# Moving similarities and transpositions in a cluster-and-convolve kernel on one core

## The chip, the cores and the metric

The kernel runs on one core of one Trainium2 chip. The metric is the device time of one execution in microseconds (us), the median of several runs. Lower is better.

## The reference

Eight images of 512 channels and 32 x 48 = 1536 pixels. Each pixel is given to the centroid (of 40) with the largest cosine similarity; each image's clusters are averaged; each pixel is pulled toward the mean of its cluster by a weight from its squared distance; a 512 x 512 matrix is applied, a bias added and ReLU taken.

```
sim = einsum('bchw,nc->bnhw', x / |x|, centroids / |centroids|)
idx = argmax(sim, axis=1);  onehot = one_hot(idx, 40)
mean = einsum('bhwn,bchw->bnc', onehot, x) / max(count, 1)
delta = mean[b, idx] - x
alpha = exp(-mean_over_channels(delta * delta))
out = relu(einsum('oc,bchw->bohw', W, x + alpha * delta) + b)
```

## The kernel before, in words

Every image is cut into three units of 512 pixels, so there are 24 units g, with image b = g // 3 and position p = g % 3. Every engine has one instruction stream, written out by hand in the order in which the engine runs it; semaphores tie the streams together. An engine that waits holds back everything behind it in its stream.

From g = 3 on, one pass of the loop over g is called a slot. Slot g of TensorE (L978) holds: `gather(g, 0)` and `gather(g, 1)` (cluster means put back on the pixels of unit g, two banks of PSUM each), four `convolve(g-2, o)` (12 matmuls each) for the unit two slots back, and `sum_squares(g)` at its end. Beside that, the next image b+1 is prepared: in the first slot of an image (p = 0) the similarities of its units 0 and 1, in the second (p = 1) those of its unit 2 and `transpose_sims`, in the third (p = 2) its cluster sums, `transpose_onehot` and `add_halves`. A slot is measured here from the start of its `gather(g, 0)` to the next.

VectorE (DVE, L515) runs in each slot: `delta(g, 0)`, the two `scale(g-1, .)`, `delta(g, 1)`, three additions in `add_squares(g)`, `fold(g)`, `low_sum(g)`. Among them stand the work for the argmax (`best_sims`, `first_best`; p = 1), for the means (`low_clusters`, `counts`, `rest_of_mean`, `parts_of_mean`; p = 2), the two-part transpositions of pixels (`transpose_half(g+4, 0)` and `(g+4, 1)`, one unit a slot), and `second_rest` (p = 0 and 1), which with GpSimd's `first_rest` splits a transposed unit into bf16 parts for the cluster sums.

ScalarE (ACT, L701) squares, copies similarities (`copy_sims`), sums and one-hots, rounds y to its high part (`high_half`), moves the upper half of the squares' sum (`move_upper`), rounds the folded sum (`high_sum`) and applies `relu`. GpSimd (POOL, L328) runs for each unit `y_half` twice, `low_half` twice, and then, for two units of three, `first_rest(g+5)`. SyncE (SP, L265) issues in each slot `store(g-3)`, `load_x(g+5)` and `load_xs(g+6)`.

Waits that matter below: `convolve(g, o)` waits until `relu(g, o-2)` has freed its half of `main` (L874); `gather(g, 1)` waits for `delta(g, 0)` (L847); `gather(g, 0)` for `add_squares(g-1)` and for the means; `transpose_half` for the cluster sums that still read the buffer it writes, and for its load; `load_xs(g)` for the transposition of unit g-2, and `load_x(g)` for `y_half` of unit g-6.

Of the kernel before, what the change touches and what calls it, by code (L numbers as in the profile page):

```python
# [21 lines left out]
Q = 4  # L22
# [13 lines left out]

SPLIT = 2

DIRECT = 2


def wait(eng, sem, value):
    if value > 0:
        eng.wait_ge(sem, value)
# [16 lines left out]


def split(g):
    return g >= 2 * PARTS and g % PARTS < SPLIT


def splits(g):
# [14 lines left out]
def build(nc, x, cent, w, bias, out):  # L82
# [3 lines left out]
    with ctx:  # L86
# [55 lines left out]

        main, gat, fa = ps("main", [P, 2, UNIT]), ps("gat", [P, 2, UNIT]), ps("fa", [P, 2, UNIT])
        al, sumP = ps("al", [P, UNIT]), ps("sump", [P, UNIT])
        simP = [fa[:, 0, 0:256], fa[:, 1, 0:256], fa[:, 0, 256:512]]
        simT = fa[:, :, :].rearrange("p a (s h n) -> p (a s h) n", h=2, n=NPAD)[:, 0:PARTS * TILES, 0:N]
        first = fa[:, 1, 384:384 + PARTS * TILES]
        ohP = fa[:, :, :].rearrange("p a n -> p (a n)").bitcast(BF16)
        def mean(b):
            return al[0:NK, :] if b == 0 else fa[0:NK, 0, :]  # L150

        def alpha(g):
            return gat[:, 0, :] if g == 1 else al[:, :]
# [30 lines left out]
        block = ctx.enter_context(nc.Block())  # L184

        def wT(k):
            return (main[:, 0, :], main[:, 1, :], gat[:, 0, :], gat[:, 1, :])[k]

        def span(g):
            return slice(g % PARTS * UNIT, (g % PARTS + 1) * UNIT)  # L190
# [146 lines left out]
        def _(dve):  # L337
            v_ = nc.vector

            def keep_transposed():  # L340
                dve.wait_ge(xp_done, 1)
                v_.tensor_copy(XT[:, 0, 0:HALF, :], main[:, :, :]).then_inc(xe_dve, 1)

            def transpose_half(g, h):
                M = C // BLK
# [70 lines left out]
            def add_squares(g):  # L416
                upper = squares(g, 1)
                dve.wait_ge(sq_done, 2 * g + 2)
                v_.tensor_tensor(SQ[:, 0, :], SQ[:, 0, :], upper[:, 0, :], ALU.add).then_inc(pair_done, 1)
                v_.tensor_tensor(upper[:, 1, :], SQ[:, 1, :], upper[:, 1, :], ALU.add).then_inc(pair_done, 1)  # L420
                dve.wait_ge(pair_done, 2 * folded(g))
                wait(dve, za_done, 2 * g)
                v_.tensor_tensor(al[:, :], SQ[:, 0, :], upper[:, 1, :], ALU.add).then_inc(s_done, 1)

            def fold(g):
# [53 lines left out]
            keep_transposed()  # L479
            best_sims(0)  # L480
            first_best(0)
            for k in range(KC):
                low_weights(k)
            transpose_half(3, 0)
            low_clusters(0)
            transpose_half(3, 1)
            counts(0)
            rest_of_mean(0)
            parts_of_mean(0)

            for g in range(DIRECT):
                delta(g, 0)
# [22 lines left out]
            for g in range(PARTS, UNITS):  # L515
                b, p = divmod(g, PARTS)
                beside = b + 1 < BATCH
                delta(g, 0)
                if g == PARTS:
                    transpose_half(g + 3, 0)  # L520
                    transpose_half(g + 3, 1)
                scale(g - 1, 0)
                scale(g - 1, 1)
                delta(g, 1)
                y_half(g - 1, 1)
                if beside and p < 2:
                    transpose_half(g + 4, 0)
                if beside and p == 2:
                    low_clusters(b + 1)
                    counts(b + 1)  # L530
                add_squares(g)
                if beside and p == 0:
                    transpose_half(g + 4, 1)
                fold(g)
                if beside and p == 2:
                    rest_of_mean(b + 1)
                if beside and p == 1:
                    best_sims(b + 1)
                low_sum(g)
                low_half(g - 1, 1)  # L540
                if beside and p == 1:
                    first_best(b + 1)
                    transpose_half(g + 4, 1)
                if beside and p == 2:
                    parts_of_mean(b + 1)
                    if g + 4 < UNITS:
                        transpose_half(g + 4, 0)
                        transpose_half(g + 4, 1)
                if g + 3 < UNITS and split(g + 3):
                    second_rest(g + 3)  # L550
            g = UNITS - 1
# [6 lines left out]
        def _(act):  # L558
            a_ = nc.scalar

            def keep_transposed(u, half):
                act.wait_ge(xp_done, 2 * u + half + 1)
                a_.activation(XT[:, u, HALF * half:HALF * (half + 1), :], (main, gat)[half][:, :, :],
                              ACT.Copy).then_inc(xe_act, 1)

            def square(g, h):
# [36 lines left out]
            def copy_sims(g):  # L603
                b, u = divmod(g, PARTS)
                act.wait_ge(sims_done, g + 1)
                wait(act, simT_done, b)
                dst, src = simS[:, u, :, :].rearrange("p t s -> p (t s)"), simP[u]
                if not plain(b):
                    dst = simS[:, u, :, :].rearrange("p t (q i) -> p q t i", q=Q)
                    src = simP[u].rearrange("p (q t i) -> p q t i", q=Q, t=HALF)  # L610
                a_.activation(dst, src, ACT.Copy, scale=cstat[:, 6:7]).then_inc(simS_done, 1)

            def copy_onehot(b):
# [51 lines left out]
            high_weights(0)  # L665
            high_weights(1)
            copy_onehot(0)
            high_weights(2)
            high_weights(3)
            copy_sums(0)  # L670
            evacuate_onehot(0)
            scale_means(0)
            high_means(0)
            act.wait_ge(b_in, 16)
            copy_sims(3)
            copy_sims(4)
# [24 lines left out]
            for g in range(PARTS, UNITS):  # L701
                b, p = divmod(g, PARTS)
                beside = b + 1 < BATCH
                if g > PARTS:
                    relu(g - 3, 3)
                    exp(g - 1)
                square(g, 0)
                if beside and p == 2:
                    copy_sums(b + 1)
                    evacuate_onehot(b + 1)  # L710
                    high_half(g - 1, 0)
                    square(g, 1)
                    high_half(g - 1, 1)
                    relu(g - 2, 0)
                    scale_means(b + 1)
                    move_upper(g)
                    high_means(b + 1)
                    high_sum(g)
                    relu(g - 2, 1)
                else:  # L720
                    relu(g - 2, 0)
                    if g == PARTS:
                        exp(g - 1)
                    square(g, 1)
                    if beside:
                        copy_sims(3 * b + 3 + 2 * p)
                    high_half(g - 1, 0)
                    if beside and p == 0:
                        copy_sims(3 * b + 4)
                    if not beside:  # L730
                        relu(g - 2, 1)
                    move_upper(g)
                    if not beside:
                        high_sum(g)
                    high_half(g - 1, 1)
                    if beside:
                        high_sum(g)
                        relu(g - 2, 1)
                relu(g - 2, 2)
                if beside and p == 1:  # L740
                    copy_onehot(b + 1)
# [13 lines left out]
        def _(pe):  # L755
            t_ = nc.tensor

            def similarities(g):
                b, u = divmod(g, PARTS)
                pe.wait_ge(x_in[b % 2][u], 16 * (b // 2 + 1))  # L760
                if b == 1:
                    pe.wait_ge(ohT_done, 1)
                wait(pe, g_ready, b if b > 1 else 0)
                if u == 2:
                    pe.wait_ge(simS_done, PARTS * b + 1)
                rows = X[b % 2]
                for k in range(KC):
                    for h in range(2):
# [2 lines left out]
                            toks = toks[:, h * HALF * P:(h + 1) * HALF * P]  # L771
                        else:
                            toks = toks.rearrange("p (q s) -> p q s", q=Q)[:, :, h * HALF * BLK:(h + 1) * HALF * BLK]
                        last = t_.matmul(simP[u][NPAD * h:NPAD * (h + 1), :], cT[:, k, :], toks,  # L774
                                         start=(k == 0), stop=(k == KC - 1))
                last.then_inc(sims_done, 1)

# [60 lines left out]
            def gather(g, h):  # L838
# [1 line left out]
                pe.wait_ge(g_ready, b + 1)  # L840
                pe.wait_ge(ohT_done, b + 1)
                if g == 0:
                    pe.wait_ge(wl_done, KC)
                elif g < DIRECT:
                    pe.wait_ge(z_done, 2 * (g - 1) + h + 1)
                elif h == 1:
# [40 lines left out]
            def transpose_x(u, half):  # L887
# [4 lines left out]
                for t in range(HALF):  # L892
                    at = u * UNIT + (HALF * half + t) * P
                    for k in range(KC):
                        last = t_.transpose((main, gat)[half][:, t, k * P:(k + 1) * P], X[0][:, k, at:at + P],
                                            ident[:, :])
                last.then_inc(xp_done, 1)

# [38 lines left out]
            transpose_weights(1)  # L937
            pe.wait_ge(const_done, 8)
            sum_clusters(0, 0)
            transpose_weights(2)  # L940
            transpose_weights(3)
            sum_clusters(0, 1)
            sum_clusters(0, 2)
            transpose_onehot(0)
            add_halves(0)

            similarities(3)
            similarities(4)
# [29 lines left out]
            for g in range(PARTS, UNITS):  # L978
# [3 lines left out]
                if beside and p == 2:  # L982
                    for u in sum_order(b + 1):
                        sum_clusters(b + 1, u)
                    gather(g, 1)
                    transpose_onehot(b + 1)
                    convolve(g - LAG, 0)
                    add_halves(b + 1)
                else:
                    convolve(g - LAG, 0)  # L990
                    if g == PARTS:
                        sum_squares(g - 1)
                    gather(g, 1)
                    if beside and p == 0:
                        similarities(3 * b + 3)
                        similarities(3 * b + 4)
                    if beside and p == 1:
                        similarities(3 * b + 5)
                convolve(g - LAG, 1)
                if beside and p == 1:  # L1000
                    transpose_sims(b + 1)
# [26 lines left out]
```

## Time and profile before

| | us |
|---|---|
| median of 3 runs (424.49 to 428.45) | 424.5 |
| the profiled execution | 424.58 |
| its span, first to last instruction | 422.8 |
| TensorE busy | 412.9 (98%) |
| VectorE busy | 344.3 (81%) |
| GpSimd busy | 263.5 (62%) |
| ScalarE busy | 256.4 (61%) |

The profiled execution took 424.58 us, 1.8 us more than its span. Busy shares are means over the whole run; a full engine is one that has no gap in the stretch looked at, and what an engine waited for stands in the table of waits.

### The profile page before, as it was taken

What the parts mean: (1) busy time and instruction counts of PE and PEld (TensorE: products, weight loads), DVE (VectorE), ACT (ScalarE), POOL (GpSimd) and SP (SyncE); (2) the same over time, 40 slices, a digit from 0 to 9 for tenths busy, and PEclk for the clock granted to TensorE, in tenths of its full rate; (3) what the DMA queues carried; (4) which work ended last, traced back from release to release, by engine and by line L of the source; (5) the groups of instructions that cost most, each with busy time, mean ns of one, the idle gap of its engine ahead of it and who ended that gap; (6) DMA issues with size and microseconds to landing.
All of it is one profiled execution on the core that took longest, in us unless ns stands there. A gap on an engine that the chain in (4) does not pass through costs nothing.

```text
span 422.8 us, 5887 instructions
## 1 busy us (share of the span) xinstructions
PE 412.9 (98%) x2154; PEld 293.7 (69%) x2154; DVE 344.3 (81%) x412; ACT 256.4 (61%) x351; POOL 263.5 (62%) x114
## 2 busy tenths in 40 slices
PE   8999999799999999999999999999999999999996
PEld 6744466575867757776777758677677758777885
DVE  2468979889799888998799997998899997788730
ACT  5665374565855666655855657747655658566641
POOL 2000655993879946995869936997669938334320
PEclk9999999899999999999999999999999999999999
DMA  8997295966669473994859674893858220222223
GB/s 276 314 292 130 51 253 153 273 169 182 215 183 240 176 200 109 258 231 142 236 119 274 175 191 160 205 292 99 207 146 246 99 101 1 101 99 99 90 79 130
DMA packets 70927, 73.94 MB, mean 175 GB/s; under 512 B 2724, under 2 KB 45732, under 8 KB 70900
## 3 DMA queue, kind: packets, MB, share of 16 engines
q1 hardware_dynamic: 70900, 73.58, 62.2%
q8 instruction: 17, 0.28, 0.3%
q14 instruction: 10, 0.08, 0.1%
HBM read 48.40 MB, written 25.17 MB: 174 GB/s over the span
## 4 chain that ended last, share of the span: by engine, by line
PE 90%; POOL 2%; DVE 2%; ACT 2%; DMA 1%; issue 1%; SPq 0%
PE main L880 20%; PE main L881 19%; PE main L882 19%; PE sump L823 9%; PE fa L774 9%; PE gat L855 5%; DMA x<-x 1%; PE fa L783 1%; PE al L862 1%; POOL z L310 1%; PE fa L798 1%; PE main L923 1%; DVE xt L350 1%; PE al L868 1%; PE gat L868 1%
## 5 line engine op out<-in xcount | busy, mean ns | idle before, releaser
L880 PE MATMUL main<-yh,wh 128*128 128x512 f32 x376 | 153.4, 408 | 2.6 <-ACT o L600 2.6
L881 PE MATMUL main<-yl,wh 128*128 128x512 f32 x376 | 147.6, 392 | 0.0
L882 PE MATMUL main<-yh,wl 128*128 128x512 f32 x376 | 147.4, 392 | 0.0
L317 POOL TENSOR_TENSOR yl<-z,yh 128x1024 fp32r<-128x1024 f32 x44 | 105.6, 2421 | 55.3 <-ACT yh L592 55.3
L310 POOL TENSOR_TENSOR z<-z,x 128x1024 f32<-128x1024 f32 x42 | 99.8, 2397 | 62.2 <-DVE z L437 62.2
L600 ACT ACTIVATE o<-main,bcol 128x512 f32<-128x512 f32 x96 | 65.0, 681 | 63.7 <-PE main L882 63.6
L880 PEld LDWEIGHTS main<-yh,wh 128*128 128x128 f32 x376 | 71.0, 189 | 23.9 <-issue 5.0
L882 PEld LDWEIGHTS main<-yh,wl 128*128 128x128 f32 x376 | 71.0, 189 | 15.3
L881 PEld LDWEIGHTS main<-yl,wh 128*128 128x128 f32 x376 | 71.0, 189 | 13.9
L324 POOL TENSOR_TENSOR xr<-xt 128x2048 f32<-128x2048 f32 x12 | 57.4, 4786 | 24.2 <-DVE xt L350 24.2
L413 DVE TENSOR_TENSOR z<-gat,x 128x1024 f32<-128x1024 f32 x46 | 56.2, 1222 | 7.5 <-PE gat L855 7.4
L592 ACT ACTIVATE yh<-z 128x1024 fp32r<-128x1024 f32 x48 | 50.6, 1054 | 10.0 <-POOL z L310 8.6
L437 DVE TENSOR_TENSOR z<-z,al 128x1024 f32<-128x1024 f32 x46 | 54.0, 1215 | 0.5 <-ACT al L587 0.5
L350 DVE STREAM_TRANSPOSE xt<-xs 128x1024 f32<-128x1024 f32 x42 | 51.0, 1230 | 0.4 <-DMA xs<-x 0.4
L774 PE MATMUL fa<-x,c_t 128*64 128x256 f32 x384 | 45.2, 383 | 0.5 <-ACT oht L623 0.3
L358 DVE TENSOR_TENSOR xr<-xr 128x2048 bf16<-128x2048 f32 x12 | 43.9, 3658 | 0.2
L574 ACT ACTIVATE sq<-z 128x1024 f32<-128x1024 f32 x22 | 23.3, 1061 | 26.4 <-DVE z L413 26.4
L774 PEld LDWEIGHTS fa<-x,c_t 128*64 128x64 f32 x384 | 26.7, 137 | 17.8 <-issue 6.9
L574 ACT ACTIVATE gat<-z 128x1024 f32<-128x1024 f32 x22 | 22.6, 1026 | 20.6 <-DVE z L413 20.6
L823 PE MATMUL sump<-xt,oh 128*64 128x512 f32 (+1 forms) x144 | 31.5, 532 | 0.0
L855 PE MATMUL gat<-oht,g 128*128 128x512 bf16 x92 | 27.9, 385 | 0.6 <-DVE g L406 0.6
L427 DVE TENSOR_TENSOR al<-upper_sum,al 64x512 f32<-64x512 f32 x22 | 15.0, 680 | 11.2 <-ACT upper_sum L578 11.2
(118 smaller groups left out, 380.0 us busy)
## 6 DMA issues: line engine op xcount, KB each, us to landing
x<-x SPq DMA_DIRECT2D x24, 1024.0 KB, 5.5
out<-o SPq DMA_DIRECT2D x23, 1024.0 KB, 6.1
xs<-x SPq DMA_DIRECT2D x84, 256.0 KB, 5.6
o<-w SPq DMA_DIRECT2D x1, 1024.0 KB, 12.1
out<-o SPq DMA_DIRECT2D x4, 256.0 KB, 2.1
sq<-centroids SPq DMA_DIRECT2D x2, 80.0 KB
bcol<-bias SPq DMA_DIRECT2D x1, 2.0 KB, 11.6
```

The source lines that it names most:

```text
L310: pool.tensor_tensor(z, z, X[g // PARTS % 2][:, pair(h), span(g)], ALU.add).then_inc(y_pool, 1)
L317: pool.tensor_tensor(YL[g % 2][:, pair(h), :], Z[g % 2][:, pair(h), :], YH[g % 2][:, pair(h), :].bitcast(F32), ALU.subtract).then_inc(lo_p ...
L324: pool.tensor_tensor(XR[:, g % PARTS, :, :].rearrange("p t c -> p (t c)"), xt.rearrange("p t c -> p (t c)"), halfword(xt, 1), ALU.subtract ...
L350: last = v_.transpose(XT[:, g % PARTS, :, :].rearrange("p t (m j) -> p m t j", j=BLK)[:, blocks, :, :], XS[g % 2][:, blocks, :])
L413: v_.tensor_tensor(Z[g % 2][:, pair(h), :], banks(g, h)[:, :, :], X[g // PARTS % 2][:, pair(h), span(g)], ALU.subtract).then_inc(z_done, 1)
L437: v_.tensor_tensor(z, z, alpha(g).unsqueeze(1).to_broadcast([P, 2, UNIT]), ALU.mult).then_inc(za_done, 1)
L600: a_.activation(OUT[g % 2][:, o, :], main[:, o % 2, :], ACT.Relu, bias=bcol[:, o:o + 1]).then_inc(relu_done, 1)
L774: last = t_.matmul(simP[u][NPAD * h:NPAD * (h + 1), :], cT[:, k, :], toks, start=(k == 0), stop=(k == KC - 1))
L823: last = t_.matmul(sumP[NPAD * h:NPAD * (h + 1), :], onehot[:, slot(u, tile), :], x_part[:, tile * C:(tile + 1) * C], start=(opens and t = ...
L880: t_.matmul(main[:, o % 2, :], WH[:, k, rows], YH[g % 2][:, k, :], start=(k == 0), stop=False)
L881: t_.matmul(main[:, o % 2, :], WH[:, k, rows], YL[g % 2][:, k, :], start=False, stop=False)
L882: last = t_.matmul(main[:, o % 2, :], WL[:, k, rows], YH[g % 2][:, k, :], start=False, stop=(k == KC - 1))
```

## The change

- From image 3 on (`AHEAD` = 9), `similarities` of unit 0 of an image run one image earlier, in the third slot between the cluster sums and `gather(g, 1)`, into the bank `al` instead of `fa`. TensorE waits for `za_done` (both `scale(g-1, .)`) before them. ScalarE's `copy_sims` of that unit stands behind `copy_sums`, and VectorE's last addition of `add_squares` waits for that copy.
- From image 3 on, the similarities of units 1 and 2 run together in the second slot, ahead of `gather(g, 1)`; none are left in the first slot. In ScalarE's second slot `copy_sims(g+3)`, `high_half(g-1, 0)`, `copy_sims(g+4)` now stand ahead of `square(g, 1)`.
- VectorE's transpositions for g+3 >= 9: none in the first slot; both halves of unit g+4 ahead of `delta(g, 1)` in the second; units g+4 and g+5 (four halves) after `parts_of_mean` in the third.
- In the first slot of every image `relu(g-2, 1)` now stands ahead of `high_sum(g)`.
- Unit 6 is no longer split (`split(g)` asks g > 6): its `first_rest` and `second_rest` go, and its cluster sums run in f32.
- At the start, the transpositions of weight blocks 2 and 3 run behind the first image's cluster sums, with ScalarE's and VectorE's copies moved accordingly; blocks 0 and 1 use `gat`, 2 and 3 `main`, and the first `gather` waits for two weight blocks instead of four.

```diff
+AHEAD = 3 * PARTS
 def split(g):
-    return g >= 2 * PARTS and g % PARTS < SPLIT
+    return g > 2 * PARTS and g % PARTS < SPLIT
+        def simP(g):
+            if g >= AHEAD and g % PARTS == 0:
+                return al[:, 0:256]
+            return (fa[:, 0, 0:256], fa[:, 1, 0:256], fa[:, 0, 256:512])[g % PARTS]
...
             # VectorE, add_squares
+                if AHEAD <= g + 4 < UNITS and g % PARTS == 2:
+                    dve.wait_ge(simS_done, g + 5)
                 v_.tensor_tensor(al[:, :], SQ[:, 0, :], upper[:, 1, :], ALU.add).then_inc(s_done, 1)
...
             # VectorE, slots
                 scale(g - 1, 1)
+                if beside and p == 1 and g + 3 >= AHEAD:
+                    transpose_half(g + 4, 0)
+                    transpose_half(g + 4, 1)
                 delta(g, 1)
                 y_half(g - 1, 1)
-                if beside and p < 2:
+                if beside and p < 2 and g + 3 < AHEAD:
                     transpose_half(g + 4, 0)
...
                 add_squares(g)
-                if beside and p == 0:
+                if p == 0 and g + 3 < AHEAD:
                     transpose_half(g + 4, 1)
                 fold(g)
...
                     parts_of_mean(b + 1)
                     if g + 4 < UNITS:
                         transpose_half(g + 4, 0)
                         transpose_half(g + 4, 1)
+                        if g + 5 >= AHEAD:
+                            transpose_half(g + 5, 0)
+                            transpose_half(g + 5, 1)
...
             # ScalarE, slots
                     copy_sums(b + 1)
+                    if AHEAD <= g + 4 < UNITS:
+                        copy_sims(g + 4)
                     evacuate_onehot(b + 1)
...
+                    elif beside and p == 1:
+                        copy_sims(g + 3)
+                        high_half(g - 1, 0)
+                        copy_sims(g + 4)
+                        square(g, 1)
...
                     move_upper(g)
                     high_half(g - 1, 1)
+                    if beside and p == 0:
+                        relu(g - 2, 1)
                     if beside:
                         high_sum(g)
+                    if beside and p == 1:
                         relu(g - 2, 1)
...
             # TensorE, similarities and slots
+                if g >= AHEAD and u == 0:
+                    pe.wait_ge(za_done, 2 * (g - PARTS - 1))
...
                         sum_clusters(b + 1, u)
+                    if AHEAD <= g + 4 < UNITS:
+                        similarities(g + 4)
                     gather(g, 1)
...
+                    if beside and p == 1 and g + 3 >= AHEAD:
+                        similarities(g + 3)
+                        similarities(g + 4)
                     gather(g, 1)
...
             # TensorE, start
             sum_clusters(0, 0)
-            transpose_weights(2)
-            transpose_weights(3)
             sum_clusters(0, 1)
             sum_clusters(0, 2)
             transpose_onehot(0)
+            transpose_weights(2)
             add_halves(0)
+            transpose_weights(3)
```

## Rows read from the trace of the kernel before

**Rows 1.** Waits of TensorE, whole run: us in total, times, longest us.

```profile
PE main L880 <- ACT o L600: 2.6, 1, 2.6
```

**Rows 2.** Busy time by window, the columns PE, PEld, DVE, ACT, POOL, clock, DMA.

```profile
80.80:85.40 4.60, 4.60 (x13) 3.48 (x13) 4.57 (x2) 0.49 (x1) 4.60 (x2) 0.63 1.12 316
...
197.70:246.30 48.60, 48.60 (x261) 34.91 (x259) 43.85 (x47) 30.69 (x43) 37.85 (x14) 1.00 0.72 195
```

**Rows 3.** The chain that ended last, 195 to 250 us: start, us, what.

```profile
197.71 0.45 PE gat L855 x2
...
202.74 0.54 PE gat L855 x2
...
215.64 0.45 PE gat L855 x2
...
219.28 3.60 PE fa L774 x32
...
231.51 0.45 PE gat L855 x2
...
235.15 1.88 PE fa L774 x16
...
246.33 0.45 PE gat L855 x2
```

**Rows 4.** Waits of VectorE from 197.7 to 246.3 us.

```profile
DVE z L413 <- PE gat L855: 0.3, 1, 0.3
```

**Rows 5.** Timeline of VectorE, slots 11 to 13: start, us, instruction.

```profile
200.21 1.20 DVE L413 TENSOR_TENSOR z<-gat,x 128x1024 f32<-128x1024 f32 x1
...
213.09 0.75 DVE L406 SCALAR_TENSOR_TENSOR g<-part,cols,fa 128x512 bf16<-128x512 bf16 x1
213.76 2.37 DVE L350 STREAM_TRANSPOSE xt<-xs 128x1024 f32<-128x1024 f32 x2
...
219.53 1.22 DVE L413 TENSOR_TENSOR z<-gat,x 128x1024 f32<-128x1024 f32 x1
...
226.25 0.68 DVE L431 TENSOR_TENSOR shl<-al,shl 64x512 fp32r<-64x512 f32 x1 [0.66 <-ACT shl L583]
226.97 4.75 DVE L358 TENSOR_TENSOR xr<-xr 128x2048 bf16<-128x2048 f32 x1
...
235.39 1.22 DVE L413 TENSOR_TENSOR z<-gat,x 128x1024 f32<-128x1024 f32 x1
...
246.37 2.56 DVE L358 TENSOR_TENSOR xr<-xr 128x2048 bf16<-128x2048 f32 x1
```

**Rows 6.** Timeline of ScalarE, slots 12 and 13.

```profile
223.89 0.60 ACT L578 ACTIVATE upper_sum<-al 64x512 f32<-64x512 f32 x1 [0.30 <-DVE al L423]
...
241.82 0.67 ACT L600 ACTIVATE o<-main,bcol 128x512 f32<-128x512 f32 x1
```

**Rows 7.** Timeline of GpSimd, slot 12.

```profile
216.21 3.60 POOL L324 TENSOR_TENSOR xr<-xt 128x2048 f32<-128x2048 f32 x1 [4.10 <-DVE xt L350]
...
224.46 4.75 POOL L317 TENSOR_TENSOR yl<-z,yh 128x1024 fp32r<-128x1024 f32 x2
229.17 5.97 POOL L324 TENSOR_TENSOR xr<-xt 128x2048 f32<-128x2048 f32 x1
```

**Rows 8.** Timeline, all engines, slot 3.

```profile
72.21 1.22 DVE L413 TENSOR_TENSOR z<-gat,x 128x1024 f32<-128x1024 f32 x1
...
73.67 4.77 POOL L310 TENSOR_TENSOR z<-z,x 128x1024 f32<-128x1024 f32 x2
...
80.77 0.50 PE L880 MATMUL main<-yh,wh 128*128 128x512 f32 x1 [2.58 <-ACT o L600]
```

**Rows 9.** Timeline of TensorE, start of the run.

```profile
22.05 1.09 PE L916 MATMUL gat<-ident,o 128*128 128x128 f32 x8
23.07 3.65 PE L823 MATMUL sump<-xt,oh 128*64 128x512 f32 x16
```

**Rows 10.** DMA issues of the page: KB each, median us to landing.

```profile
x<-x SPq DMA_DIRECT2D x24, 1024.0 KB, 5.5
```

More of the change, by code:

```diff
@@ L144, in build @@
         al, sumP = ps("al", [P, UNIT]), ps("sump", [P, UNIT])
-        simP = [fa[:, 0, 0:256], fa[:, 1, 0:256], fa[:, 0, 256:512]]
         simT = fa[:, :, :].rearrange("p a (s h n) -> p (a s h) n", h=2, n=NPAD)[:, 0:PARTS * TILES, 0:N]
@@ L186, in wT @@
         def wT(k):
-            return (main[:, 0, :], main[:, 1, :], gat[:, 0, :], gat[:, 1, :])[k]
+            return (gat[:, 0, :], gat[:, 1, :], main[:, 0, :], main[:, 1, :])[k]
         def span(g):
@@ L341, in keep_transposed @@
                 dve.wait_ge(xp_done, 1)
-                v_.tensor_copy(XT[:, 0, 0:HALF, :], main[:, :, :]).then_inc(xe_dve, 1)
+                v_.tensor_copy(XT[:, 0, 0:HALF, :], gat[:, :, :]).then_inc(xe_dve, 1)
             def transpose_half(g, h):
@@ L481, in _ @@
             first_best(0)
-            for k in range(KC):
-                low_weights(k)
+            low_weights(0)
+            low_weights(1)
             transpose_half(3, 0)
@@ L487, in _ @@
             counts(0)
+            low_weights(2)
             rest_of_mean(0)
             parts_of_mean(0)
+            low_weights(3)
             for g in range(DIRECT):
@@ L542, in _ @@
                     first_best(b + 1)
-                    transpose_half(g + 4, 1)
+                    if g + 3 < AHEAD:
+                        transpose_half(g + 4, 1)
                 if beside and p == 2:
@@ L562, in keep_transposed @@
                 act.wait_ge(xp_done, 2 * u + half + 1)
-                a_.activation(XT[:, u, HALF * half:HALF * (half + 1), :], (main, gat)[half][:, :, :],
+                a_.activation(XT[:, u, HALF * half:HALF * (half + 1), :], (gat, main)[half][:, :, :],
                               ACT.Copy).then_inc(xe_act, 1)
@@ L606, in copy_sims @@
                 wait(act, simT_done, b)
-                dst, src = simS[:, u, :, :].rearrange("p t s -> p (t s)"), simP[u]
+                dst, src = simS[:, u, :, :].rearrange("p t s -> p (t s)"), simP(g)
                 if not plain(b):
                     dst = simS[:, u, :, :].rearrange("p t (q i) -> p q t i", q=Q)
-                    src = simP[u].rearrange("p (q t i) -> p q t i", q=Q, t=HALF)
+                    src = simP(g).rearrange("p (q t i) -> p q t i", q=Q, t=HALF)
                 a_.activation(dst, src, ACT.Copy, scale=cstat[:, 6:7]).then_inc(simS_done, 1)
@@ L667, in _ @@
             copy_onehot(0)
-            high_weights(2)
-            high_weights(3)
             copy_sums(0)
             evacuate_onehot(0)
+            high_weights(2)
             scale_means(0)
             high_means(0)
+            high_weights(3)
             act.wait_ge(b_in, 16)
@@ L723, in _ @@
                         exp(g - 1)
-                    square(g, 1)
-                    if beside:
+                    if g + 3 < AHEAD:
+                        square(g, 1)
                         copy_sims(3 * b + 3 + 2 * p)
-                    high_half(g - 1, 0)
-                    if beside and p == 0:
-                        copy_sims(3 * b + 4)
+                        high_half(g - 1, 0)
+                        if p == 0:
+                            copy_sims(3 * b + 4)
+                    elif beside and p == 1:
+                        copy_sims(g + 3)
+                        high_half(g - 1, 0)
+                        copy_sims(g + 4)
+                        square(g, 1)
+                    else:
+                        square(g, 1)
+                        high_half(g - 1, 0)
                     if not beside:
@@ L762, in similarities @@
                     pe.wait_ge(ohT_done, 1)
-                wait(pe, g_ready, b if b > 1 else 0)
+                if g >= AHEAD and u == 0:
+                    pe.wait_ge(za_done, 2 * (g - PARTS - 1))
+                else:
+                    wait(pe, g_ready, b if b > 1 else 0)
                 if u == 2:
@@ L773, in similarities @@
                             toks = toks.rearrange("p (q s) -> p q s", q=Q)[:, :, h * HALF * BLK:(h + 1) * HALF * BLK]
-                        last = t_.matmul(simP[u][NPAD * h:NPAD * (h + 1), :], cT[:, k, :], toks,
+                        last = t_.matmul(simP(g)[NPAD * h:NPAD * (h + 1), :], cT[:, k, :], toks,
                                          start=(k == 0), stop=(k == KC - 1))
@@ L842, in gather @@
                 if g == 0:
-                    pe.wait_ge(wl_done, KC)
+                    pe.wait_ge(wl_done, KC // 2 * (h + 1))
                 elif g < DIRECT:
@@ L894, in transpose_x @@
                     for k in range(KC):
-                        last = t_.transpose((main, gat)[half][:, t, k * P:(k + 1) * P], X[0][:, k, at:at + P],
+                        last = t_.transpose((gat, main)[half][:, t, k * P:(k + 1) * P], X[0][:, k, at:at + P],
                                             ident[:, :])
@@ L992, in _ @@
                         sum_squares(g - 1)
+                    if beside and p == 1 and g + 3 >= AHEAD:
+                        similarities(g + 3)
+                        similarities(g + 4)
                     gather(g, 1)
[L994 to L998, printed above, removed]
+                    if p == 0 and g + 3 < AHEAD:
+                        similarities(g + 3)
+                        similarities(g + 4)
+                    if p == 1 and g + 3 < AHEAD:
+                        similarities(g + 4)
                 convolve(g - LAG, 1)
```

## The prediction

> **What bounds the kernel now.** First the table of TensorE's waits: it waits in earnest once, 2.6 us [rows 1], so from the first slots to the end the time is the sum of its matmuls. Then the windows of one image, slots 11 to 13: TensorE busy in all of 48.60 us, at the full clock, VectorE in 43.85 [rows 2]. That looks like 4.8 us to spare on VectorE, and the next view takes it back: in those 48.6 us VectorE waits for TensorE only 0.3 us, at one `delta` [rows 4]. The rest of its idle time it waits for ScalarE, which in those places works on what VectorE gave it a moment before; this is a chain that no faster TensorE shortens. So VectorE's stream with its hand-overs to ScalarE is nearly as long as TensorE's. The change leaves the work of both as it is and moves it; the question is whether VectorE still fits.
>
> **The slots by TensorE alone.** From the chain [rows 3]: the third slot 215.64 - 197.71 = 17.9 us, the first 231.51 - 215.64 = 15.9, the second 246.33 - 231.51 = 14.8, together 48.6. Two units of similarities cost 3.60, one unit 1.88. After the change TensorE would need 17.9 + 1.9 = 19.8 in the third slot, 15.9 - 3.6 = 12.3 in the first, 14.8 - 1.9 + 3.6 = 16.5 in the second: the same 48.6. Nothing is gained there; waits can only be added. VectorE has the most to do in the first and second slots.
>
> **The third slot after.** VectorE enters it 200.21 - 197.71 = 2.5 us late, busy with `second_rest` [rows 3, 5]. Its `delta` and two `scale` take 3.4 (from the end of the transpositions at 213.76 + 2.37 = 216.13 to the next `delta` at 219.53 [rows 5]). The added wait of TensorE for the second `scale` ends at 2.3 + 3.4 = 5.7 into the slot (2.3 is the lateness that comes out below), while the cluster sums are done at 202.74 - 197.71 = 5.0 [rows 3]: 0.7 us of waiting, with `gather(g, 1)`, the one-hot transpositions and all convolutions queued behind. What follows on ScalarE and VectorE starts from these, so it shifts by 1.9 + 0.7 = 2.6, as does the slot's end: 20.5 us. `parts_of_mean` now ends about 213.84 - 197.71 = 16.1 in [rows 3, 5], then at 18.7, still 1.8 before the slot's end. ScalarE's added copy lies in the time in which it waits for the one-hots, and VectorE's added wait for that copy is over long before: nothing for both. The early similarities need their pixels: these are issued after `y_half` in the second slot, some 10 us in by the walk below, and land 5.5 later [rows 10], before the third slot begins. Nothing for that. The transposed loads of SyncE are no later, since the transpositions that release them come earlier or in the same place.
>
> **The first slot after** (t from its start). VectorE has four halves of transpositions instead of two behind `parts_of_mean`: 4 x 1.18 = 4.7 (2.37 for two [rows 5]), from t = -1.8 to 2.9. Now `delta(g, 0)` comes at 2.9 instead of 0.5, and `gather(g, 1)`, due at 3.2, waits until 4.1. `delta(g, 1)` starts at 2.9 + 3.4 = 6.3. From there to `move_upper` it is 223.89 - 219.53 = 4.4 [rows 5, 6]. Before, two halves of transpositions lay in this stretch, yet their removal shortens nothing: they lay beside ScalarE's square and move, which now show as waits of VectorE. `move_upper` starts at 10.7; behind it in ScalarE's stream stand `high_half` and then `relu(g-2, 1)`, together to 12.8 (0.6, 1.05 and 0.68, less overlaps of their starts; in slot 13 `move_upper`, `high_half`, `high_sum` and this `relu` end 7.1 after `delta(g, 1)`, 241.82 + 0.67 - 235.39 [rows 5, 6], of which `high_sum` is 0.6). Convolution 3 waits for that `relu`. By TensorE it would be due at 10.0, so it waits 2.8, and the slot ends after it and `sum_squares`, 3.0 later: 15.9 us instead of 12.3. The 3.6 us taken out of the slot come back whole.
>
> Meanwhile VectorE does `low_sum` to 14.05 and then `second_rest`. In the trace that takes 2.56 alone and 4.75 when GpSimd is in its `low_half` [rows 5]: there it ended at 231.72, 2.55 after GpSimd's pair ended at 224.46 + 4.75 = 229.2, and GpSimd's `first_rest`, begun then, took 5.97 instead of 3.60 [rows 7]. The two take turns. GpSimd here has `first_rest` from 0.6 to 4.2, two `y_half` to 9.9, two `low_half` (2.37 each, half of 4.75) to 14.7. So `second_rest` ends at 14.7 + 2.55 = 17.25, 1.4 into the second slot.
>
> **The second slot after.** `delta`, `scale` and two halves of transpositions (5.8) bring VectorE to 7.2; `gather(g, 1)`, now behind 3.6 of similarities, gives `delta(g, 1)` at 7.3 instead of 3.9. `relu(g-2, 1)` here still stands behind `high_sum`, so it ends 7.1 later, at 14.4. Convolution 3 is due at 13.6: it waits 0.8, and the slot is 17.4. The argmax and `second_rest` (alone, 2.56) end 19.7 in, so 2.3 into the third slot, which closes the circle.
>
> One image: 20.5 + 15.9 + 17.4 = 53.8 against 48.6, or 5.2 more. Five images run so (third slots 5 to 17, with the first and second after each): 5 x 5.2 = +26.
>
> **The start.** In slot 3 GpSimd's `first_rest(6)` kept `y_half(2)` off until 73.67, its `high_half` and a `relu` came behind, and TensorE waited 2.58 until 80.77 [rows 8]. Without it, and with `relu` ahead of `high_sum`, the limit is ScalarE's stream: `delta` at 72.21 [rows 8] + 4.4 + 2.1 = 78.75, 2.0 earlier; I take 1.9. In the 4.6 us behind the wait the clock was 0.63 of full [rows 2]: matmuls at 1.2 GHz for most of it, 4.6 x 0.37 = 1.7 lost. I take that back, as 0.7 us of waiting remains; bounds 0 and 1.7. Unit 6 in f32: two f32 units 3.65 [rows 9], so 1.85 a unit; the sums of three units now 202.74 - 198.16 = 4.6 [rows 3], so 1.37 a split unit: +0.5. The weight transpositions took 23.07 - 22.05 = 1.0 between cluster sums [rows 9]; moved behind them, they let the first means come earlier, less a weight copy of 0.55 on ScalarE in the same path. I take 0.7, bounds 0 and 1.0. Sum: -1.9 - 1.7 + 0.5 - 0.7 = -3.8.
>
> **The clock.** Each first slot after has a wait of about 2.8 us, near to the one of 2.58 behind which the clock fell, at a cost of 1.7 [rows 1, 2]. Whether each of the five does so, one row can't tell: 0 to 1.7 each; I take half, +4. Total: 424.6 - 3.8 + 26 + 4 = 451 us. The median equals the profiled run within 0.1 us.
>
> **Rivals.**
> - VectorE fits, and TensorE stays the bound: only the start counts, 424.6 - 3.8 = 420.8, faster by 0.9%. For it: TensorE's work is unchanged, and 4.8 us of VectorE stand idle in an image [rows 2]. Against it: the four halves would have to end by about the first slot's start, so `parts_of_mean` 4.2 before it, and it ends 1.8 before. Chance 0.07.
> - VectorE's lateness is absorbed, and only the order on GpSimd and ScalarE binds. `first_rest` ends at 4.2 into the first slot, the second `y_half` at 8.9, `high_half` and `relu` at 10.6; convolution 3, due at 9.1, waits 1.5. With 0.8 in the second slot and 0.7 in the third it is 3.0 an image: 420.8 + 15 = 436. Chance 0.15.
> - The turns of `second_rest` and `first_rest` go the other way. If the second `low_half` ends before `low_sum` (0.6 us of margin above), GpSimd starts `first_rest` (3.6) and VectorE waits for all of it: 20.2 instead of 17.25, which puts `delta(g, 1)` of the second slot 2.9 later: 5 x 2.9 = 14.5, so 465. Chance 0.1. The Trainium skill (SBUF — State Buffer, Who interferes with whom) says that a VectorE instruction with two SBUF inputs contends with a GpSimd one that reads SBUF, and that issue order decides who blocks, wholly. By that rule, this rival is decided by which is first, and the turns in the trace agree.
> - The forecast, with both ends of the clock's cost: 447 to 456. Chance 0.65; 0.03 is left for what I do not see.
>
> From the second rival's 436, less 2 for the start's bounds, to 461, between the forecast's end and the third rival, the range holds 8 in 10. A change under 1% can hardly be told from none here. Faster than that: 0.04, half of the first rival and a little of the start's bounds; within 1%: 0.05; slower: 0.91.
>
> **What would show it.** Right: chain pieces of `gather` that make first slots near 15.9 us, not 12.3; TensorE waits of 2 to 3 us at convolution 3 behind a `relu`, five times; VectorE without a wait for TensorE in the first slot; its `delta(g, 0)` there some 3 us after the slot's start; slot 3 shorter by about 3.6. Wrong: images of 48.6 us, a `delta` in the first slot that waits for `gather`, or third slots much beyond 20.5, which would mean pixels that come late. The weakest links are 2.8 us of waiting (it decides on the clock) and the turns of the two bf16 splits.

## The result and the profile after

The changed kernel takes 453.2 us, median of 6 runs (450.8 to 455.9), against 424.8 us for the kernel before, run beside it: a ratio of 1.065, 95% interval 1.060 to 1.070. The forecast was 451, the range 434 to 461. The profiled execution is the fastest of the six, 450.77 us with a span of 449.0.

TensorE's waits, whole run (us in total, times, longest), answer to [rows 1]:

```profile
PE main L917 <- ACT o L619: 19.2, 11, 2.7
PE gat L892 <- DVE z L420: 3.6, 5, 0.7
PE al L810 <- DVE z L447: 2.7, 5, 0.7
```

One wait of 2.6 us has become 21 waits, in three places, each once an image for five images: `convolve` for `relu` (eleven: one in slot 3, and two an image), `gather(g, 1)` for a late `delta`, and the early similarities for the second `scale`.

Two images by window, slots 8 to 10 and 11 to 13 (TensorE, its weight loads, VectorE, ScalarE, GpSimd, clock, DMA share, GB/s), answer to [rows 2]:

```profile
150.90:204.90 54.00, 48.73 (x255) 35.12 (x259) 42.33 (x47) 30.36 (x43) 37.80 (x14) 1.00 0.65 175
204.90:260.40 55.50, 50.21 (x255) 36.18 (x259) 42.46 (x47) 30.39 (x43) 37.79 (x14) 0.97 0.65 174
```

54.0 us instead of 48.6 for the same matmuls; TensorE stands idle 5.3. No engine is full any more: here the time goes along a chain that passes from engine to engine. The second image took 1.5 more at a lower clock.

TensorE's timeline, the starts of `gather(g, 0)` of slots 8 to 11 and the waits between (start, us, instruction), answers to [rows 3]:

```profile
150.91 0.38 PE L892 MATMUL gat<-oht,g 128*128 128x512 bf16 x1
...
156.39 1.95 PE L810 MATMUL al<-x,c_t 128*64 128x256 f32 x16 [0.52 <-DVE z L447]
...
171.29 0.38 PE L892 MATMUL gat<-oht,g 128*128 128x512 bf16 x1
...
175.13 0.59 PE L892 MATMUL gat<-oht,g 128*128 128x512 bf16 x2 [0.72 <-DVE z L420]
...
183.84 0.50 PE L917 MATMUL main<-yh,wh 128*128 128x512 f32 x1 [2.65 <-ACT o L619]
...
187.16 0.38 PE L892 MATMUL gat<-oht,g 128*128 128x512 bf16 x1
...
201.62 0.50 PE L917 MATMUL main<-yh,wh 128*128 128x512 f32 x1 [1.05 <-ACT o L619]
...
204.94 0.38 PE L892 MATMUL gat<-oht,g 128*128 128x512 bf16 x1
```

The third slot takes 171.29 - 150.91 = 20.4, the first 15.9, the second 17.8. The first slot holds 3.6 us less work than before and is as long as before.

VectorE's timeline through that first slot, from the transpositions behind `parts_of_mean` on, answers to [rows 5]:

```profile
169.26 4.61 DVE L357 STREAM_TRANSPOSE xt<-xs 128x1024 f32<-128x1024 f32 x4
173.80 1.18 DVE L420 TENSOR_TENSOR z<-gat,x 128x1024 f32<-128x1024 f32 x1
174.91 2.33 DVE L447 TENSOR_TENSOR z<-z,al 128x1024 f32<-128x1024 f32 x2
177.17 1.21 DVE L420 TENSOR_TENSOR z<-gat,x 128x1024 f32<-128x1024 f32 x1
179.47 0.69 DVE L426 TENSOR_TENSOR sq<-sq,gat 128x512 f32<-128x512 f32 x1 [1.10 <-ACT gat L593]
...
182.16 0.69 DVE L437 TENSOR_TENSOR al<-upper_sum,al 64x512 f32<-64x512 f32 x1 [0.66 <-ACT upper_sum L597]
...
184.29 0.68 DVE L441 TENSOR_TENSOR shl<-al,shl 64x512 fp32r<-64x512 f32 x1 [1.45 <-ACT shl L602]
185.01 3.10 DVE L365 TENSOR_TENSOR xr<-xr 128x2048 bf16<-128x2048 f32 x1
```

The four halves end 2.5 us after the slot's start, the first `delta` begins there instead of 0.5 in, and the two places where halves of transpositions lay before, beside ScalarE's square and move, now show as VectorE's waits (1.10 and 0.66). The third wait, 1.45, is for `high_sum`, ahead of which a `relu` now stands. ScalarE's and GpSimd's lines of the same slot, answers to [rows 6] and [rows 7]:

```profile
181.53 0.59 ACT L597 ACTIVATE upper_sum<-al 64x512 f32<-64x512 f32 x1 [1.11 <-DVE al L433]
182.03 1.04 ACT L611 ACTIVATE yh<-z 128x1024 fp32r<-128x1024 f32 x1
183.10 0.69 ACT L619 ACTIVATE o<-main,bcol 128x512 f32<-128x512 f32 x1
```

```profile
180.92 4.67 POOL L324 TENSOR_TENSOR yl<-z,yh 128x1024 fp32r<-128x1024 f32 x2
185.56 5.97 POOL L331 TENSOR_TENSOR xr<-xt 128x2048 f32<-128x2048 f32 x1
```

The `relu` that ends at 183.79 is what convolution 3 waited for, and it stood behind `move_upper`, which waited 1.11 for VectorE's last addition.

### The profile page after: what moved, and what is told of

Same layout as the page of the kernel before. It is cut to its first block, busy times and chain, and to the rows that moved or that the text cites. A ratio compares the mean times of both kernels' runs of the same rounds, so it can differ in the third digit from the quotient of the medians.

```text
span 449.0 us, 5849 instructions
## 1 busy us (share of the span) xinstructions
PE 413.7 (92%) x2123; PEld 294.8 (66%) x2150; DVE 332.2 (74%) x411; ACT 254.4 (57%) x351; POOL 257.4 (57%) x113
## 4 chain that ended last, share of the span: by engine, by line
PE 47%; DVE 28%; ACT 13%; issue 10%; DMA 1%; SPq 0%; ACTq 0%; DVEq 0%
PE main L917 9%; PE main L918 8%; PE main L919 8%; PE fa L810 7%; DVE z L447 6%; DVE xt L357 5%; ACT yh L611 5%; DVE z L420 5%; PE sump L859 3%; ACT gat L593 3%; PE gat L892 3%; DVE xr L365 3%; PE al L810 2%; DVE al L433 2%; DVE gat L427 2%
## 5 line engine op out<-in xcount | busy, mean ns | idle before, releaser
L917 PE MATMUL main<-yh,wh 128*128 128x512 f32 x376 | 156.2, 415 | 19.2 <-ACT o L619 19.2
L918 PEld LDWEIGHTS main<-yl,wh 128*128 128x128 f32 x376 | 71.5, 190 | 13.9
L331 POOL TENSOR_TENSOR xr<-xt 128x2048 f32<-128x2048 f32 x11 | 51.4, 4675 | 23.9 <-DVE xt L357 23.9
L357 DVE STREAM_TRANSPOSE xt<-xs 128x1024 f32<-128x1024 f32 x42 | 49.4, 1219 | 2.6 <-DMA xs<-x 2.6
L810 PE MATMUL fa<-x,c_t 128*64 128x256 f32 x304 | 35.5, 383 | 0.8 <-DMA x<-x 0.8
L365 DVE TENSOR_TENSOR xr<-xr 128x2048 bf16<-128x2048 f32 x11 | 31.2, 2835 | 0.2
L426 DVE TENSOR_TENSOR sq<-sq,gat 128x512 f32<-128x512 f32 x22 | 15.1, 686 | 20.6 <-ACT gat L593 20.6
L810 PEld LDWEIGHTS fa<-x,c_t 128*64 128x64 f32 x304 | 21.0, 137 | 13.6 <-issue 4.3
L892 PE MATMUL gat<-oht,g 128*128 128x512 bf16 x65 | 21.7, 381 | 6.6 <-DVE z L420 3.6
```

The lines of the kernel that those rows point to most:

```text
L357: last = v_.transpose(XT[:, g % PARTS, :, :].rearrange("p t (m j) -> p m t j", j=BLK)[:, blocks, :, :], XS[g % 2][:, blocks, :])
L810: last = t_.matmul(simP(g)[NPAD * h:NPAD * (h + 1), :], cT[:, k, :], toks, start=(k == 0), stop=(k == KC - 1))
L917: t_.matmul(main[:, o % 2, :], WH[:, k, rows], YH[g % 2][:, k, :], start=(k == 0), stop=False)
L918: t_.matmul(main[:, o % 2, :], WH[:, k, rows], YL[g % 2][:, k, :], start=False, stop=False)
```

## Experiments

Times are medians; each is beside runs of the kernel before on the same chip (424.6 to 424.8).

**The two halves of the change, apart and without both.** Four kernels make a square: neither (`start_only`), similarities alone, transpositions alone, and the changed kernel with both.

```diff
-AHEAD = 3 * PARTS
+AHEAD = UNITS          # start_only
```

> Keeps the change at the start, unit 6 unsplit and relu ahead of high_sum in first slots; similarities and transpositions stay where they were. My theory: the start is worth 3.8 us and nothing else is left, 420.8 us. Rival (the loss sits in what this kernel keeps, such as the order of relu in every first slot): above 430.

421.1 us (ratio 0.992, 0.990 to 0.993): TensorE's only wait for another engine beyond the start is 0.7 us in slot 3. So what the changed kernel loses comes from the two moves.

```diff
+MOVED = UNITS          # sims_only; the conditions on VectorE's transpositions test MOVED for AHEAD
...
+AHEAD = UNITS          # transpositions_only
+MOVED = 3 * PARTS
```

> The changed kernel with the transpositions where they were. Theory (late VectorE is one half of the loss): the first slot falls from 15.9 to 13.8 (convolution 3 waits 1.5 behind relu, second y_half and first_rest), the second stays at 17.8, the third waits 1.5 for the second scale and takes 21.3; 52.9 an image, 420.8 + 5 x 4.3 = 442. Rival A (the four halves are the whole cause): 421 to 424. Rival B (they are no cause): 450.

445.8 us (1.050, 1.049 to 1.052). TensorE's waits:

```profile
PE main L918 <- ACT o L620: 16.4, 11, 1.6
PE al L811 <- DVE z L448: 5.6, 5, 1.2
PE sump L860 <- DVE xt L358: 1.7, 5, 0.3
```

The convolutions of the first slot wait 1.57, as expected from `first_rest` and `y_half`, but those of the second 1.6 and not 1.05: there `square(g, 1)` stands behind `high_half(g-1, 0)`, and GpSimd is late with the `y_half` that this one needs. So the similarities alone cost 24.7 us over `start_only`, 3.5 more than I had worked out.

> The changed kernel with the similarities where they were, transpositions moved. Theory: third slot 17.9; first slot 15.9 + 0.9 (gather 1 waits for a late delta) = 16.8 with no wait at convolution 3; second slot: delta 1 at 6.3 instead of 3.9, convolution 3 waits 1.6, 16.4; 51.1 an image, 420.8 + 5 x 2.5 = 433. Rival A (transpositions alone do it): about 450. Rival B (similarities alone do it): 421.

433.6 us (1.022, 1.020 to 1.023). The slots take 17.9, 16.7 and 16.6, close to what was expected, but the waits are not all those named: convolution 3 of the second slots waits 0.8 and not 1.6, and `transpose_sims` waits 0.4 for ScalarE's copy.

```profile
PE main L918 <- ACT o L620: 4.8, 6, 0.8
PE gat L893 <- DVE z L421: 3.5, 5, 0.7
PE fa L820 <- ACT sims L631: 2.0, 5, 0.4
```

Transpositions alone cost 12.5, similarities alone 24.7, both 32.1 (453.2 - 421.1). But in the last number the clock fell, and in the other two it stayed full. In the profiled execution of the changed kernel these falls cost 2.8 us; without them both moves cost 450.8 - 2.8 - 421.1 = 26.9, and the parts, 37.2 together, are 10 us more than the whole, since the same slots are late in both. The image of slots 8 to 10 says the same: 48.6 us with neither move (145.70 to 194.32), 51.2 with the transpositions (147.75 to 198.94), 53.7 with the similarities (149.62 to 203.34), 54.0 with both. The similarities are most of the loss. On top of them the transpositions add little to an image; they lengthen the longest wait from 1.6 to 2.65 us, and it is behind such waits that the clock fell. So the rivals that put all on the transpositions fall, and so does the one that put nothing on them when they are moved alone. The rival of `sims_only` that they are no cause, 450, is off by 4.2, and the theory's 442 by 3.8: that run alone does not tell them apart.

**Is the order on ScalarE the cause?**

```diff
-                    if not beside:
+                    if not beside or g + 3 >= AHEAD:
                         relu(g - 2, 1)
                     move_upper(g)
...                  # the later call of this relu goes in these slots
```

> The changed kernel with relu(g-2, 1) ahead of move_upper in the first and second slots of images 3 to 7, so that convolution 3 no longer waits behind VectorE's additions. Theory (VectorE's chain is the bound, relu is only where TensorE feels it): first slot 13.1, but VectorE then starts the second slot 4 us late, and it and the third slot take back what was won; 53.5 an image, 448 to 450. Rival (the order on ScalarE is the cause): 2.7 + 1.05 us saved in each of five images, 432.

445.4 us (1.049, 1.048 to 1.051); the image takes 53.6 us (148.40 to 202.02), as expected, and 421 + 5 x 4.9 gives 445. The 448 to 450 was reckoned from the changed kernel's median, in which falls of the clock are contained; here the clock stayed full. TensorE now waits for VectorE by name:

```profile
PE sump L859 <- DVE oh L386: 7.5, 5, 1.5
PE al L810 <- DVE z L447: 6.1, 5, 1.4
PE gat L892 <- DVE z L420: 3.5, 5, 0.7
PE al L899 <- DVE shl L441: 2.4, 5, 0.5
```

3.7 us of waits for `relu` an image are gone, and the image is 0.4 us shorter: TensorE stands idle 4.7 us of it instead of 5.3, most of that in these four places. Of the 7.8 us between the two medians about 5 are falls of the clock that are gone. The order on ScalarE was where TensorE felt the chain; VectorE was the chain.

**Ahead of the gather, or behind it?** Similarities moved, transpositions not, but the similarities run behind `gather(g, 1)`.

```diff
+                    gather(g, 1)
                     if AHEAD <= g + 4 < UNITS:
                         similarities(g + 4)
-                    gather(g, 1)
```

(The same in the second slot, and there `square(g, 1)` ahead of the copies on ScalarE.)

> As sims_only (similarities moved, transpositions where they were), but in the third and second slots the similarities run behind gather(g, 1), and square(g, 1) ahead of their copies. Theory (what costs in the similarities' move is that VectorE waits for a gather that stands behind them): second slot 16.5 without a wait at convolution 3, first slot 13.8, third 20.6; 50.9 an image, 420.8 + 11.7 = 433. Rival A (unequal slots alone cost it, the place within the slot does not matter): 445. Rival B (the place is all of it): 421.

431.8 us (1.017, 1.015 to 1.018). Of the 24.7 us that the similarities cost alone, 14 go with the place within the slot. VectorE's waits for a gather, whole run, first in `sims_only`, then here:

```profile
DVE z L421 <- PE gat L893: 30.6, 15, 2.7
...
DVE z L421 <- PE gat L893: 8.1, 7, 2.6
```

So the matmuls ahead of the gather were a wait of VectorE for its `delta`. What the order on ScalarE, changed with it, has in the 14 was not separated. Most of the rest is the first slot, which takes 13.9 us, since convolution 3 still waits 1.57:

```profile
PE main L918 <- ACT o L620: 8.6, 6, 1.6
```

**That last wait, with `relu` ahead of `move_upper` in first slots.**

> As sims_behind_gather, with relu(g-2, 1) ahead of move_upper in first slots, so that convolution 3 there (1.57 us of waiting in each of five) is free. Theory: VectorE and GpSimd begin the second slot later by the same amount; its convolution 3 waits about 0.8: 427. Rival (the wait was the order on ScalarE alone): 431.8 - 7.9 = 424.

434.3 us (1.021, 1.019 to 1.024): slower than without it, and neither number was right. The wait left convolution 3 and came back larger, in a place that I had not reckoned with:

```profile
PE gat L891 <- DVE z L421: 9.8, 5, 2.0
```

With a first slot of 12.05 us VectorE comes out of `second_rest` so late, 3.9 us into the second slot (184.50 - 180.61), that `gather(g, 1)` there waits for `delta(g, 0)`. At the full clock nothing is won or lost by that: three slots take 50.8 us (168.57 to 219.36), as in `sims_behind_gather` (147.23 to 197.99). What makes this kernel slower is the clock, which fell behind two of the five waits: those second slots take 20.4 and 20.3 us instead of 18.7, a loss of 3.3 us; less 1.0 won in slot 3 that makes 2.3 of the 2.5 us between the medians.

**The terms of the start.** The kernel before with one part each: unit 6 unsplit; `relu` ahead of `high_sum` in first slots; weights' transpositions moved.

> The kernel before with unit 6 unsplit, nothing else. Theory (first_rest of unit 6 on GpSimd held the chain of slot 3): relu of slot 3 still behind high_sum, 0.5 later than in the changed kernel, so convolution 3 waits 1.25 instead of 2.6; the clock does not fall (1.7); f32 sums cost 0.5: 424.6 - 2.5 = 422.1. Rival (the order of relu was the cause): 425.

> The kernel before with relu(g-2, 1) ahead of high_sum in first slots, nothing else. Theory: with first_rest still ahead of y_half in slot 3, the wait there shrinks by 0.6 to about 2.0; all other first slots had no wait. 424.0, or 422.3 if the clock does not fall behind the shorter wait. Rival (the order of relu was the cause): 421.5.

> The kernel before with the moved transpositions of weights, nothing else. Theory: first gather 0.7 earlier, but slot 3 begins only 0.5 earlier: 424.0 to 424.1. Rival (hidden by the chain through VectorE): 424.6.

422.4 (0.994, 0.993 to 0.996), 424.2 (0.999, 0.998 to 1.000) and 424.0 us (0.998, 0.998 to 0.999): -2.3, -0.5 and -0.7, together the -3.5 of `start_only`. In `split_only` the wait in slot 3 is 1.4 us and the clock stays full; in `relu_only` it is 2.1 and the clock still falls, in 9 of 11 executions by their mean clocks.

**A faster start.** What is left in slot 3 is 0.7 us for a `relu`; ahead of `move_upper` it should go.

```diff
-                    if not beside:
+                    if not beside or p == 0:      # start_relu_early; g == PARTS: start_relu_slot3
                         relu(g - 2, 1)
                     move_upper(g)
...                  # the later call of this relu goes in these slots
```

> As start_only, with relu(g-2, 1) ahead of move_upper in first slots. Theory: the last 0.74 us of waiting in slot 3 goes, all other slots have no wait: 420.4. Rival (VectorE's chain in slot 3 gives it back): 421.1.

424.7 us: 3.6 slower than `start_only`, against both expectations. `start_relu_early_look` is the same kernel once more, for its trace (424.6 us), and `start_relu_slot3` has the edit in slot 3 alone.

> start_relu_early once more, for its trace. Theory: relu, now ahead of move_upper, waits for convolution 1, which runs behind 3.6 us of similarities in the first slot; so move_upper, fold and low_sum come some 2 us later, GpSimd has started first_rest before VectorE reaches second_rest, and VectorE waits for all of it; gather(g, 1) of the second slot then waits for a late delta. 424.7, with second_rest ending 2.5 us after first_rest. Rival: the loss is in slot 3 alone.

> As start_only, with relu(g-2, 1) ahead of move_upper in slot 3 alone, where no second_rest follows. Theory: 0.7 us of waiting goes, 420.4. Rival (the loss of start_relu_early is in slot 3): 424.

`start_relu_slot3`: 420.0 us (0.989, 0.987 to 0.990), the fastest of all; its interval just meets that of `start_only`. So the loss is in the other first slots. ScalarE, VectorE and GpSimd in one of them, slot 12, which starts at 212.66:

```profile
223.05 0.69 ACT L619 ACTIVATE o<-main,bcol 128x512 f32<-128x512 f32 x1 [2.17 <-PE main L917]
223.77 0.60 ACT L597 ACTIVATE upper_sum<-al 64x512 f32<-64x512 f32 x1
```

```profile
224.40 0.69 DVE L437 TENSOR_TENSOR al<-upper_sum,al 64x512 f32<-64x512 f32 x1 [2.20 <-ACT upper_sum L597]
...
226.68 3.62 DVE L365 TENSOR_TENSOR xr<-xr 128x2048 bf16<-128x2048 f32 x1
```

```profile
225.39 2.41 POOL L324 TENSOR_TENSOR yl<-z,yh 128x1024 fp32r<-128x1024 f32 x1 [1.26 <-ACT yh L611]
227.75 5.97 POOL L331 TENSOR_TENSOR xr<-xt 128x2048 f32<-128x2048 f32 x1
```

Half of the theory holds: with similarities behind the gather, convolution 1 is late, `relu` waits 2.17 for it in front of everything else on ScalarE, and VectorE's `fold` waits 2.20 behind that. The other half does not: `second_rest` still got its turn before `first_rest`. VectorE enters the second slot at 230.3, 1.8 late, and TensorE waits 0.2 at a convolution there and 0.3 at the cluster sums of the third slot, in five images:

```profile
PE sump L857 <- DVE xt L357: 1.6, 5, 0.3
PE main L915 <- ACT o L619: 1.1, 5, 0.2
```

These waits add up to 2.7 us, and the slots show more. From one first slot to the next it is 49.6 us (178.95 to 228.53) and not 48.6 (179.50 to 228.12): second slots are 0.55 longer and third ones 0.42, 4.8 in five images. Slot 3, from the `sum_squares` before it to its own, is 1.05 shorter, which leaves 3.8, against 3.6 between the medians. A wait in these tables counts from the end of the matmul before, as the profile models it: `start_only` shows 0.74 in slot 3, and the slot is 1.05 shorter without it.

## Why the prediction was right, step by step

- TensorE as the bound of the kernel before, with VectorE just below it: right. `start_only` runs the old slots with no wait behind slot 3, and each kernel that moved similarities or transpositions takes 11 to 32 us more than it, with the same matmuls for TensorE.
- Third slot 20.5: measured 20.4. The wait for `scale` was put at 0.7 and is 0.5.
- First slot 15.9: measured 15.9. `gather(g, 1)` was to wait 0.9, and waits 0.7; convolution 3 was to wait 2.8, and waits 2.65. That the sum is exact is luck: `relu` ends 12.5 into the slot and not 12.8, and what stands behind it takes 3.4 and not 3.0.
- Second slot 17.4: measured 17.8, with 1.05 of waiting at convolution 3 instead of 0.8. This is the term furthest off, and small: `relu` ends 14.4 in, as put, and again it is the 3.0 behind it that is 3.4. `second_rest` ended at 188.1, 0.95 into the slot and not 1.4, and 2.5 after GpSimd's `low_half` ended, as the turns were read.
- One image 53.8: measured 54.0, so +27 for five, where +26 was put.
- The start -3.8: the changed kernel enters slot 5 about 4.0 earlier than the kernel before; `start_only` gives -3.5, and its parts -2.3 (put at -2.5 by the same rows), -0.5 and -0.7. One term in it is not settled, the 1.7 us for a fall of the clock in slot 3. The traces bear it out (17.2 us with the fall and a wait of 2.58, 14.4 in `split_only` without the fall and with a wait of 1.36), but the times do not: of 52 executions of the kernel before beside the experiments, the 36 with a mean clock of 0.995 or 0.996 have a median of 424.8 us, and the 16 with 0.999 or 1.000 one of 424.65. What cost those 16 the same time is open, since no trace of one was kept.
- The clock: half of five falls at 1.7, +4. In the profiled execution it fell in two of the five first slots, 12 and 18, which took 17.3 and 17.2 instead of 15.9: +2.8. The six runs have mean clocks from 0.981 to 0.992 and times from 455.9 to 450.8 in the same order, so the rest of the difference to the median is more such falls; that is read from the means, not from a trace of each run. Half of five was a choice, not a reading, and that it came out close is luck. That the median would equal the profiled run within 0.1 us, as it did before, did not hold: it lies 2.4 above it.
- Sum for the profiled execution: -4.0 at the start, +27 waits, +2.8 clock and +0.5 for unit 6 in f32 make +26.3; measured 450.8 - 424.6 = 26.2. (The unit's 0.5 was in the -3.8.)
- The rivals: "TensorE stays the bound" fell with the first windows. "Only the order on GpSimd and ScalarE binds" is right in `sims_only` and `sims_behind_gather` for its 1.5 us in the first slot (1.57 measured), but not in the changed kernel, where VectorE is later still. Its 3.0 an image is too little even for `sims_only`, where an image takes 5.1 more: there VectorE waits for the gather behind the similarities (up to 2.7 us at a time), and the four halves, by which the prediction explains the first slot, are not needed for most of the loss. The turns of the bf16 splits went the same way in every trace: `second_rest` began before the second `low_half` ended, by 0.6 to 2.3 us. So the condition of the third rival never came about, and its price is not tested.

## What to carry to other kernels

An engine that is full hides how close the next one is: before making a slot shorter for the full engine, walk the slot for the second one, hand-overs included, because work moved out of a wait leaves the wait behind and still has to be done elsewhere. Where a wait for one engine's result is removed by reordering, ask what was late on the others. Three times here the wait came back under another name: `relu_early` won 0.4 of 3.7 us an image, `sims_behind_gather_relu_early` nothing, and `start_relu_early` lost 1.0 an image. And price the parts of a change apart: this one held 3.5 us of gain in its start, which alone, with one more `relu` moved, gives 420.0 us.

## What the runs showed of the hardware

The clock does not fall behind every long wait. Behind five waits of 2.63 to 2.66 us in the changed kernel it fell twice; first the window of slot 12 from before its wait to its end, then the same of slot 9, where it did not:

```profile
234.50:242.60 8.10, 5.42 (x17) 3.79 (x17) 5.42 (x5) 3.49 (x6) 8.10 (x4) 0.79 0.82 213
...
180.80:187.10 6.30, 3.64 (x15) 2.48 (x15) 4.16 (x4) 3.49 (x6) 6.30 (x4) 1.00 0.82 231
```

It fell behind 2.1 us in `relu_only`, behind two of five waits of 1.96 to 1.98 in `sims_behind_gather_relu_early` (20.4 and 20.3 us for a second slot of 18.7), and never in `sims_only` behind ten waits of 1.5 to 1.6. For these waits of 2.0 to 2.7 us a share of the falls is all that could be forecast.

VectorE's `second_rest` and GpSimd's `low_half` take turns. In the first slots of all traces `second_rest` ended 2.4 to 2.5 us after the running `low_half`, whether it began 0.6 us before that end (3.1 us long in the changed kernel) or 2.2 (4.7 in the kernel before). Alone it takes 2.5 to 2.6. So the longer durations in the profile hold a wait, not slower work.
